# First token tiles of an attention and MLP kernel: rotation ahead of two statistics, two small loads ahead of x

## What is computed

```python
x = x + attn(layernorm(x))      # 16 heads of 32
x = x + ffn(layernorm(x))       # 512 -> 4096 -> 512, gated, weights in 4-bit codes

# attn: linear attention with decay, chunks of 128 tokens
q, k, v = x @ Wq, x @ Wk, x @ Wv
q, k = rotate(silu(q)), rotate(silu(k))
scores = einsum('bthd,bshd->bhts', q, k) * D          # inside a chunk
o = scores @ v + (q * decay_q) @ S                    # S: state carried over chunks
S = lam_C * S + (k * decay_k).T @ v
o = group_rmsnorm(o * sigmoid(x @ Wg1 @ Wg2)) * weight
return o @ Wo
```

## Time and profile before

| | |
|---|---|
| median of 3 runs | 1390.36 us (1389.65 to 1391.3) |
| the profiled execution | 1391.3 us |
| its span, first to last instruction | 1389.3 us |
| around the span | 2.0 us |
| mean granted TensorE clock | 0.997 |
| TensorE busy | 1361.1 us (98% of the span) |
| VectorE busy | 1053.3 us (76%) |
| ScalarE busy | 417.6 us (30%) |
| GpSimd busy | 244.3 us (18%) |

### The profile page before, as it was taken

One profiled execution on the slowest core, in us unless ns is written; L12 is line 12 of the kernel. 1 busy time (PEld: TensorE's weight loads), 2 busy tenths in 40 slices (PEclk: granted clock), 3 DMA queues, 4 the chain that ended last, 5 costly groups with the idle time before them and its releaser, 6 DMA issues.

```text
span 1389.3 us, 18724 instructions
## 1 busy us (share of the span) xinstructions
PE 1361.1 (98%) x7132; PEld 1122.5 (81%) x7132; DVE 1053.3 (76%) x1698; ACT 417.6 (30%) x669; POOL 244.3 (18%) x136
## 2 busy tenths in 40 slices
PE   8899999997999999999999999999999999999999
PEld 5788888886788888888888888888888888888887
DVE  7899998886677676868686867777776868686845
ACT  5333443332232222222232222222222222222221
POOL 1444444451110110101011101010110101010100
PEclk9999999999999999999999999999999999999999
DMA  9000000000000000100000100000000000000002
GB/s 320 22 1 1 17 16 16 1 1 1 16 31 16 31 31 16 31 15 30 15 30 27 34 15 30 15 30 15 30 28 17 30 15 30 15 30 16 1 31 91
DMA packets 21783, 40.29 MB, mean 29 GB/s; under 512 B 2661, under 2 KB 2917, under 8 KB 21605
## 3 DMA queue, kind: packets, MB, share of 16 engines
q1 hardware_dynamic: 21060, 39.47, 8.6%
q10 hardware_dynamic: 672, 0.13, 0.0%
HBM read 35.40 MB, written 4.19 MB: 29 GB/s over the span
## 4 chain that ended last, share of the span: by engine, by line
PE 94%; DVE 3%; issue 1%; ACT 1%; DVEq 0%; ACTq 0%
PE bank L948 29%; PE bank L950 29%; PE bank L949 29%; PE bank L962 2%; PE bank L1038 1%; PE bank L1055 1%; PE bank L1187 1%; PE bank L1045 1%; DVE x1l L709 1%; PE bank L1066 0%; PE bank L1005 0%; PE bank L1004 0%; PE bank L1017 0%; DVE acc L800 0%; DVE hl L834 0%
## 5 line engine op out<-in xcount | busy, mean ns | idle before, releaser
L948 PE MATMUL bank<-x1h,wh 128*128 128x512 f32 x1024 | 398.9, 390 | 1.4 <-DVE x1l L709 1.4
L949 PE MATMUL bank<-x1l,wh 128*128 128x512 f32 x1024 | 398.5, 389 | 0.0
L950 PE MATMUL bank<-x1h,wl 128*128 128x512 f32 x1024 | 398.4, 389 | 0.0
L882 POOL TENSOR_TENSOR wl<-wf,wh 128x1024 fp32r<-128x1024 f32 x48 | 114.9, 2395 | 856.9 <-ACT wh L377 856.9
L948 PEld LDWEIGHTS bank<-x1h,wh 128*128 128x128 f32 x1024 | 192.4, 188 | 41.5 <-issue 1.6
L949 PEld LDWEIGHTS bank<-x1l,wh 128*128 128x128 f32 x1024 | 192.4, 188 | 40.0
L950 PEld LDWEIGHTS bank<-x1h,wl 128*128 128x128 f32 x1024 | 192.3, 188 | 39.9
L809 DVE SCALAR_TENSOR_TENSOR hx<-hx,bank 128x512 f32<-128x512 f32 x128 | 87.9, 687 | 156.6 <-ACT hx L461 156.6
L948 PE MATMUL bank<-wh,hh 128*128 128x512 f32 x512 | 200.6, 392 | 3.2 <-DVE x1l L709 3.2
L949 PE MATMUL bank<-wl,hh 128*128 128x512 f32 x512 | 200.4, 391 | 0.0
L950 PE MATMUL bank<-wh,hl 128*128 128x512 f32 x512 | 200.4, 391 | 0.0
(11 more groups left out here) (117 smaller groups left out, 1476.2 us busy)
## 6 DMA issues: line engine op xcount, KB each, us to landing
pk<-packed_dram SPq DMA_DIRECT2D x48, 256.0 KB
sc<-scales_dram SPq DMA_DIRECT2D x48, 256.0 KB
out_dram<-acc SPq DMA_DIRECT2D x16, 256.0 KB, 2.1
acc<-x_dram SPq DMA_DIRECT2D x3, 1024.0 KB, 13.5
w_in<-wq_dram SPq DMA_DIRECT2D x2, 512.0 KB, 4.8
w_in<-wk_dram SPq DMA_DIRECT2D x2, 512.0 KB, 6.5
w_in<-wv_dram SPq DMA_DIRECT2D x2, 512.0 KB, 8.2
w_in<-wo_dram SPq DMA_DIRECT2D x2, 512.0 KB, 10.9
```

The costliest lines, as they stand in the source:

```text
L882: nc.gpsimd.tensor_tensor(wl[par][:, bass.ds(u, 1), :].rearrange("p a w -> p (a w)"), wf[:].rearrange("p a w -> p (a w)"), wh[par][:, bass ...
L948: pe.matmul(dst, w_h, x_h, start=start, stop=False)
L949: pe.matmul(dst, w_h, x_l, start=False, stop=False)
L950: return pe.matmul(dst, w_l, x_h, start=False, stop=stop)
```

## The change

Three programs are reordered; no instruction is added or dropped. SyncE issues Wg2 and the rotation table before tiles 2 and 3 of x. ScalarE makes the high part of Wg2 after `xt_hi_(1)`, `tanh_qk(0)` and `gate_low(0)` instead of before them. VectorE makes the low part of tile 1's x, silu and gate of tile 0 first, then the low part of Wg2, then its half of the rotation of tile 0, and only then the statistics of tiles 2 and 3, both steps of them.

```diff
@@ SyncE
             load_w(2, 2)
-            sp.dma_start(acc[:, 2:CHUNKS, :], xv[:, 2:CHUNKS, :]).then_inc(s_x[0], 16)
             sp.dma_start(g2_in, wg2.unsqueeze(0).broadcast_to([4, HD, 512])).then_inc(s_g2, 16)
             sp.dma_start(rotT[:], rot).then_inc(s_rot, 16)
+            sp.dma_start(acc[:, 2:CHUNKS, :], xv[:, 2:CHUNKS, :]).then_inc(s_x[0], 16)
             load_x(1)
@@ ScalarE
             weight_hi(2, 2, 1)
-            act.wait_ge(s_g2, 16)
-            A(g2s[:], g2_in, ACT.Copy).then_inc(s_ghi, 1)
             xt_hi_(1)
             tanh_qk(0)
             gate_low(0)
+            act.wait_ge(s_g2, 16)
+            A(g2s[:], g2_in, ACT.Copy).then_inc(s_ghi, 1)
             v_copy(0, 0)
@@ VectorE
             weight_lo(2, 2, 1)
+            xt_lo_(1)
+            silu_qk(0)
+            gate_low(0)
             dve.wait_ge(s_ghi, 2)
             V.tensor_tensor(g2s[32:64, :], g2_in[32:64, :], g2s[32:64, :].bitcast(F32),
                             ALU.subtract).then_inc(s_glo, 1)
-            xt_lo_(1)
+            dve.wait_ge(s_rot, 16)
+            rope_of(None, 0, 0, 0)
             dve.wait_ge(s_x[0], 16)
             stats(2, 4)
-            silu_qk(0)
-            gate_low(0)
             stats_r(2, 4, 1)
-            dve.wait_ge(s_rot, 16)
-            rope_of(None, 0, 0, 0)
             dve.wait_ge(s_x[1], 16)
             stats(4, 2 * CHUNKS)
```

## The result

The changed kernel took 1397.41 us in the median of six runs (1394.74 to 1398.28), the kernel before 1390.62 beside it: a ratio of 1.0046, interval 1.0036 to 1.0057, so 6.4 us slower (5.0 to 7.9). I had forecast the right sign, 1393.3 us, and a range that ended at 1394.8. The profiled execution took 1397.07 us, its span 1395.3, which is 6.0 above the span before.

The account below looks back on a forecast made before the run. TensorE, busy 98% of the span, was taken as the bound. Scores 2.0 us later plus 0.9 at half clock made 2.9 us: 1394.2 for the profiled execution, 1393.3 against the median; range 1389.5 to 1394.8.

Parts of the forecast that it names:

- The front part and the rotation: Start of the kernel: gate matmul 1.7 us earlier, at 21.9; rotation 3.5 us earlier, GpSimd's addition ending at 28.0.
- the loads give nothing: SyncE's three reordered transfers: no effect on the time, with 1.4 us of cover for tiles 2 and 3.
- The statistics: VectorE's newton steps for tiles 2 and 3: 2.7 us later, done at 30.65, held by GpSimd's long instructions.
- The third step: Newton step on VectorE, held by GpSimd's addition until 28.0; by the trace alone the least sure of three stalls.
- nearly no loss: Claim for newton without the stall from GpSimd's addition: leaving it out would give 28.3.
- The queue behind the statistics: ScalarE's norm of tile 2 at 30.7 delays tanh_qk(1) to 33.95, scores to 37.4: 2.0 us later.
- The clock: TensorE at half clock after 4.7 us of idling: the 32 score matmuls take 0.9 us more.
- The 2.1 for q: Up to 2.1 us more if the half clock reaches the 12 matmuls of q of tile 2.
- rival 4: Half clock covers scores and q, or tiles 2 and 3 land past 23.0: 4 to 6 later, to 1396; chance 0.07.
- Rival 1: Stalls come but the clock stays, or kd misses newton: 1.2 to 2.0 later, 1391.6 to 1392.4; chance 0.24.
- The sum: Whole kernel: 2.0 for late scores plus 0.9 for half clock, 2.9 us slower, 1393.3 against the median.
- Faster, or no change: Two rivals: newton escapes GpSimd, scores 1.8 us earlier, 1388.6, chance 0.14; or within 0.5 us of before, chance 0.07.

Follow-up runs that it names:

- the old order of loads: The changed kernel with SyncE again loading tiles 2 and 3 of x ahead of the gate weight and the rotation table: 1396.14 us, ratio 1.0038.
- Wo ahead of the norm: The changed kernel with Wo's high part moved ahead of tile 2's norm on ScalarE: 1393.42 us, ratio 1.0018; run again 1393.88 us, 1.0017.
- the kernel with nothing of tile 1 behind the statistics: The changed kernel with tile 1's tanh, silu and gate and Wo's high part ahead of norm and later bn_stats: 1388.34 us, ratio 0.9984.
- The filled pause: The changed kernel with three small matmuls on zeros between the transposes and q of tile 2: 1393.88 us, ratio 1.0028.
- the filled idle stretch: The changed kernel with four matmuls on zeros on TensorE between v of tile 1 and the scores of tile 0: 1393.02 us, ratio 1.0009.

## Why the prediction was right and wrong

**The front part and the rotation: right.** Gate matmul forecast at 21.9, measured 21.89; addition forecast to end at 28.0, measured 28.05, and the transposes behind it no longer wait. That the loads give nothing here was right too, shown by the old order of loads; taken alone they are worth 1.4 us at the scores.

**The statistics: right.** Forecast 30.65, measured 30.61, by three steps held to the ends of rb, addition and kd. That GpSimd holds them is shown by the kernel in which its addition waits: the same VectorE program with two of the three stalls gone. By the Trainium skill (SBUF — State Buffer, Who interferes with whom) the one that issues second is blocked for the whole instruction; the trace agrees, with 2.30 us for a 0.16 us step. The third step, which I called the least sure, is held by the addition as forecast. One number beside it was wrong: without that hold the steps would end by 27.7 (25.5 and eleven of 0.20), ahead of `kd`, and not at 28.3, so that the scores would come some 1.0 us earlier than before and not "nearly no loss". Where the addition waits, the shift is out at 27.74. More hung on this one stall than I wrote.

**The queue behind the statistics: right.** Norm 30.65 for 30.7, tanh 33.82 for 33.95, scores 37.50 for 37.4. Shown by Wo ahead of the norm (1.9 us back) and by the kernel with nothing of tile 1 behind the statistics (all of it and 2.1 more).

**The clock: this term failed.** That a spell would come was right, its length was not. I had it over the scores alone, 0.9 us, on the ground that it would run out before q of tile 2. It lasted 10.2 us, in both traces of the changed kernel, and took 3.4: 0.92 at the scores, 0.46 at the transposes, 2.06 at q. The transposes I had put at nothing without a reason. The 2.1 for q stood in the prediction as a bound and as rival 4, at 0.07. My reason, that the spell runs on and out while ScalarE and VectorE prepare q, did not hold in the changed kernel: TensorE stood 1.46 us there and came back to q at half clock. The course that I forecast does occur, once with Wo ahead of the norm (3.4 us, over before q), but the same kernel had 10.2 us in its other trace. The filled pause (6.8 us) suggests that standing still there lengthens the spell. What decides its length stays open. What the clock cost as a whole is shown by the filled idle stretch, 3.4 us in the trace and 3.5 to 4.4 in the medians. Rival 1, as far as it built on the 3.25 us of the earlier trace rows that had no fall, lost: 5.00, 3.14 and even 1.47 us of idling went with one.

**The sum.** 2.0 + 0.9 should have been 2.1 + 3.4 = 5.5 at tile 1's scores; with 0.5 in the late spells, for which the sum had no term, that is the 6.0 of the span. The range ended at 1394.8, though the prediction's own upper price for the clock, 2.1 more than the forecast, gives 1395.4. Even rival 4's 1396 lies below the measured 1397.41.

**Faster, or no change: lost.** newton did not escape GpSimd, and what the front part won turned into idle time of TensorE.

## What to carry to other kernels

Before an operation is moved ahead on one engine, write down which engine will run beside what is left behind: tiny dependent steps next to another engine's long instructions on SBUF can take that engine's time, not their own (2.30 us for 0.16 here). When a stage loses time on a path that TensorE waits for, price the idle stretch and then the matmuls behind it at half clock, as a range: once for the first group alone, once for all up to the next long unbroken run of matmuls. Here one program had both. And read who queues behind the late value on the same engine; here most of the work that waited did not need it.

## What was not expected of the hardware

A spell at half clock followed 1.47 us of idle TensorE (at 30.4) in one kernel, while 3.25 us in another place brought none. After the same idle 3.14 us in the same program the spell was 3.4 us in one execution and 10.2 in another. With three small matmuls in a pause of 1.46 us it was 6.8 us long, in three traces with that pause and 5.00 us of idling 10.2. Where exactly it begins and what ends it is left open. The runs show that its length is no fixed number, and that work put into the idle stretch ahead can keep the spell away.
